# POOL splits one table part behind its first four lookups, and the indices of the lookups move to ACT's queue

## The reference

```python
e = jnp.stack([tbl_0[ids[:, 0]], ..., tbl_39[ids[:, 39]]], axis=1)      # (512, 40, 32)
iidx, jidx = jnp.triu_indices(40, k=1)                                  # 780 pairs
z = jnp.einsum('bpd,pde,bpe->bp', e[:, iidx, :], bilinear_matrices, e[:, jidx, :])
h = jnp.concatenate([z, dense_ctx], axis=1)                             # (512, 796)
h = jnp.maximum(h @ W_top1 + b_top1, 0.0)                               # 512
h = jnp.maximum(h @ W_top2 + b_top2, 0.0)                               # 256
y = h @ W_top3                                                          # (512, 1)
```

## Time and profile before

| | |
|---|---|
| Median of 3 runs | 193.12 us (193.04 to 193.39) |
| The profiled execution's own time | 193.5 us |
| Its span in the trace | 191.7 us |
| Granted TensorE clock in the span | 1.0 of full speed |
| Busy: PE | 179.4 us (94%) |
| Busy: DVE | 147.5 us (77%) |
| Busy: POOL | 107.0 us (56%) |
| Busy: ACT | 52.9 us (28%) |

### The profile page before, as it was taken

How to read it: one execution, slowest core, us unless ns; L and a number is a source line. 1 busy time by engine, 2 the same in 40 slices (tenths; PEclk the granted TensorE clock), 3 DMA queues, 4 the chain that set the end, 5 groups by cost and what they waited for, 6 DMA issues and landing times.

```text
span 191.7 us, 3810 instructions
## 1 busy us (share of the span) xinstructions
PE 179.4 (94%) x1630; PEld 57.9 (30%) x1630; DVE 147.5 (77%) x147; ACT 52.9 (28%) x52; POOL 107.0 (56%) x114
## 2 busy tenths in 40 slices
PE   6688598899999999999999999999999999998992
PEld 6433232233313222222232223222222323222340
DVE  1899989997689979668699969686969987663502
ACT  3879496894100210211110111102011011112501
POOL 2678777878777777777777777779020002222000
PEclk9999999999999999999999999999999999999999
DMA  5995212340397410140000000000000000000000
GB/s 142 390 392 222 67 43 33 94 120 12 84 319 261 148 20 14 26 153 13 14 14 17 14 12 15 14 14 10 2 0 3 0 0 0 3 0 2 3 0 0
DMA packets 7609, 12.89 MB, mean 67 GB/s; under 512 B 2068, under 2 KB 4504, under 8 KB 7592
## 3 DMA queue, kind: packets, MB, share of 16 engines
q1 hardware_dynamic: 4520, 11.07, 16.9%
q0 software_dynamic: 3072, 1.58, 4.6%
HBM read 12.64 MB, written 0.00 MB: 66 GB/s over the span
## 4 chain that ended last, share of the span: by engine, by line
PE 86%; DVE 7%; DMA 2%; issue 2%; ACT 1%; DVEq 0%
PE ps_t L637 29%; PE ps_z L651 26%; PE ps_x L675 11%; PE ps_t L631 5%; PE ps_t L686 4%; DVE hot_dve L516 4%; PE ps_x L601 4%; PE ps_t L601 3%; DMA ids<-ids_oh 2%; PE ps_t L660 2%; DVE late_w L523 2%; PE ps_x L613 2%; PE ps_z L601 1%; DVE tbl_last L526 1%; DVE prod L556 1%
## 5 line engine op out<-in xcount | busy, mean ns | idle before, releaser
L556 DVE TENSOR_TENSOR prod<-ps_t,xt 128x1024 f32<-128x1024 f32 x100 | 115.7, 1217 | 25.5 <-PE ps_t L637 22.1
L446 POOL DMA_INDIRECT emb<-tbl,idx x96 | 95.8, 998 | 32.8 <-issue 29.0
L637 PE MATMUL ps_t<-xt,w_sb 32*128 32x512 f32 x360 | 58.6, 640 | 0.0
L651 PE MATMUL ps_z<-prod,ones 128*32 128x512 f32 x400 | 53.0, 604 | 0.0
L454 POOL TENSOR_TENSOR late_z<-late_z,tbl_oh 128x512 f32<-128x512 f32 x8 | 10.1, 1279 | 36.2 <-ACT tbl_oh L497 36.2
L637 PEld LDWEIGHTS ps_t<-xt,w_sb 32*128 32x128 f32 x360 | 19.8, 183 | 34.2 <-issue 21.0
L675 PE MATMUL ps_x<-late_z,late_w 128*32 128x512 f32 x192 | 22.8, 592 | 0.0
L516 DVE TENSOR_SCALAR hot_dve<-ids,ramp 128x2048 bf16<-128x2048 int16 x26 | 18.1, 745 | 3.7 <-DMA ids<-ids_oh 3.7
L651 PEld LDWEIGHTS ps_z<-prod,ones 128*32 128x32 f32 x400 | 8.1, 108 | 37.9 <-issue 31.0
L469 ACT ACTIVATE hot_act<-ids,neg_ramp 128x2048 bf16<-128x2048 int16 x8 | 15.9, 1992 | 3.0 <-DMA ids<-ids_oh 3.0
L497 ACT ACTIVATE tbl_oh<-ps_x 128x512 f32<-128x512 f32 x8 | 4.8, 597 | 40.7 <-PE ps_x L675 40.7
(11 more groups left out here) (62 smaller groups left out, 86.8 us busy)
## 6 DMA issues: line engine op xcount, KB each, us to landing
ids<-ids_oh SPq DMA_DIRECT2D x4, 512.0 KB, 7.0
emb<-tbl,idx POOLq DMA_INDIRECT x96, 2.4
late_w<-w SPq DMA_DIRECT2D x1, 1280.0 KB, 10.3
tbl_oh<-small_tables SPq DMA_DIRECT2D x2, 512.0 KB, 8.7
late_w<-w SPq DMA_DIRECT2D x2, 512.0 KB, 4.9
w_sb<-w_pairs SPq DMA_DIRECT2D x1, 704.0 KB
tbl_oh<-small_tables SPq DMA_DIRECT2D x1, 640.0 KB
w_sb<-w_pairs SPq DMA_DIRECT2D x1, 640.0 KB
```

The costliest lines, as they stand in the source:

```text
L446: nc.gpsimd.indirect_dma_start(emb[:, n % E_RING, t, u * D:(u + 1) * D], None, tables[field], bass.IndirectOffsetOnAxis(ap=idx[:, at:at + ...
L556: nc.vector.tensor_tensor(prod[:, g % PROD_RING, :].rearrange("p (i b) -> p i b", i=2), ps_t[PAIR[g]][:, :].rearrange("p (i b) -> p i b", ...
L637: last = nc.tensor.matmul(o, w_sb[s * D:(s + 1) * D, at:at + P], xt[s * D:(s + 1) * D, kk, :], start=True, stop=True)
L651: last = nc.tensor.matmul(ps_z[q * D:(q + 1) * D, :], ones[:, v * D:(v + 1) * D], prod[:, t // 2 % PROD_RING, t % 2 * B:(t % 2 + 1) * B], ...
```

## The change

Four things change.

- The two subtractions of table part 3 move from DVE to POOL, which does them behind its fourth lookup, when the part has landed. They have semaphores of their own, `tbl_rest_pool` and `tbl_last_pool`, and PE waits for the latter ahead of hot (2, 0).
- DVE splits part 4 behind the step hot (2, 3), and no longer behind hot (2, 7).
- The load of `idx` is issued by ACT, as its first instruction, and no longer by SP.
- The counts of the waits are renumbered, since DVE makes four parts.

```diff
+POOL_PART, POOL_LOOKUPS = 3, 4
+DVE_PARTS = [n for n in range(len(TBL_PARTS)) if n != POOL_PART]
...
-SPLIT_AT = {(0, 3): 1, (1, 3): 2, (2, 7): 3}
+SPLIT_AT = {(0, 3): 1, (2, 3): 3}
...
             load_small_ids(0)
-            sp.dma_start(idx[:, :], ids).then_inc(ids_in, 16)
             load_small_tables(0)
...
+            def split_part():
+
+                cols = part_cols(POOL_PART)
+                pool.wait_ge(tbl_in[POOL_PART], 16)
+                nc.gpsimd.tensor_tensor(tbl_rest[:, cols], tbl_oh[:, cols], upper_halves(tbl_oh[:, cols]),
+                                        ALU.subtract).then_inc(tbl_rest_pool, 1)
+                pool.wait_ge(tbl_rest_pool, 1)
+                nc.gpsimd.tensor_tensor(tbl_last[:, cols], tbl_rest[:, cols], upper_halves(tbl_rest[:, cols]),
+                                        ALU.subtract).then_inc(tbl_last_pool, 1)
+
             pool.wait_ge(ids_in, 16)
+            lookups = 0
             for n, k in enumerate(looked_up):
...
                             bass.IndirectOffsetOnAxis(ap=idx[:, at:at + 1], axis=0)).then_inc(gathered[k], 16)
+                        lookups += 1
+                        if lookups == POOL_LOOKUPS:
+                            split_part()
...
+            act.dma_start(idx[:, :], ids).then_inc(ids_in, 16)
             act.wait_ge(ramp_made, len(OH_BLOCKS))
...
-                dve.wait_ge(tbl_rest_made, n + 1)
+                dve.wait_ge(tbl_rest_made, DVE_PARTS.index(n) + 1)
...
-                        pe.wait_ge(tbl_last_made, PART_OF_BLOCK[j] + 1 if j else 1)
+                        if PART_OF_BLOCK[j] == POOL_PART:
+                            pe.wait_ge(tbl_last_pool, 1)
+                        else:
+                            pe.wait_ge(tbl_last_made, DVE_PARTS.index(PART_OF_BLOCK[j]) + 1 if j else 1)
```

More of the change, by code:

```diff
@@ L346, in dlrm_tower @@
         tbl_rest_made, tbl_last_made = sem("tbl_rest_made"), sem("tbl_last_made")
+        tbl_rest_pool, tbl_last_pool = sem("tbl_rest_pool"), sem("tbl_last_pool")
         hot_made_dve, hot_made_act = sem("hot_made_dve"), sem("hot_made_act")
```

## The result

The changed kernel takes 198.68 us (median of 4 runs, 197.25 to 199.39), the kernel before 193.19 us beside it; ratio 1.027 (95% interval 1.024 to 1.031), 5.2 us slower by the ratio. The forecast was 198.0 us. The profiled execution of after is the shortest of the four: 197.25 us, span 195.4 us, 3.7 us more than before. The other three lie at 198.57 to 199.39 us, at a mean granted clock of 0.981 to 0.983. None of these three left a trace; the experiments come back to this gap.

The account below looks back on a forecast made before the run. PE sets the pace from 31.7 us; before that a chain through DVE binds. DVE held 2 x 2.4 us plus 0.1 us gives 193.5 + 4.9 = 198.4 us, less 0.4 us for the median: 198.0 us, range 193.3 to 199.0 us.

Parts of the forecast that it names:

- What bounds, and what is late next: Block 2: PE's 1.93 us wait for DVE is no prize, since ACT's one-hot pair ends at 30.15 us, PE's meeting 30.20.
- The exclusion: Block 1's start: DVE stands for the whole of both POOL subtractions, 4.8 us, read from POOL's lookups standing behind DVE.
- Rivals 1 and 2: 1: POOL does not hold DVE up, 192.8 to 194.3 us, chance 0.25; 2: DVE goes first, 196.1 to 198.6 us, 0.08.
- rival 3: Partial: only one subtraction excludes, or accesses are dealt out in turn; +1 to +3.5 us, 194.1 to 196.6 us, chance 0.09.
- the fourth: Table lands so late that POOL works behind block 1's one-hots, around 20 us; +2 to +5 us, no chance of its own.
- the sum: Block 1: two DVE one-hots held 2.4 us each plus 0.1 us handing over, 4.9 us late, carried to the end.
- POOL's duration: POOL's two 128x1024 subtractions: 2.4 us each, 4.8 us together, from a range of 2.25 to 2.56 us.
- the sign that the prediction named: Profile after: POOL's two 128x1024 instructions of 2.3 to 2.6 us begin at the end of a DVE instruction.
- The indices: Load on ACT's queue: earlier indices gain 0, sharing engines with the first ids costs at most 0.4 us; taken as 0.
- The argument of equal bytes: Indices and first ids at the head are the same bytes together, so moving the load's issue was taken as 0.
- The band of 197.3 to 198.8 us: Forecast case for the whole kernel, said to follow from POOL's 2.25 to 2.56 us; chance 0.58.
- What moves along: Part 4's early split has 0.5 to 1 us of cover, block 3's lookups 2 us; PE's wait on POOL's part 0.

Follow-up runs that it names:

- the half-size run: Against the kernel with only the split on POOL: POOL's two subtractions made on 128x512, PE reading the first half's for the second half; 195.09 us, ratio 1.009.
- the later place: Against the kernel with only the split on POOL: POOL's split put behind its tenth lookup in place of its fourth; 196.78 us, ratio 1.018.
- the spare matmuls: Kernel with only the split on POOL, plus 10 and 4 identity matmuls on PE ahead of one-hot matmuls (1, 0) and (1, 1); 197.15 us, ratio 1.022.
- the kernel with ACT relieved: Kernel in which nobody splits part 3, with DVE making one-hot (2, 3) in place of ACT; 191.78 us, then 190.82 us with part 4's split put back late.
- both split: Kernel before, DVE making every split, with POOL repeating the two subtractions into tiles nobody reads; 198.43 us, ratio 1.025.

## Why the prediction was right

**What bounds, and what is late next.** Right, and shown in both directions: no split of part 3 at all gives 0.9996, with PE standing for ACT's pair; with ACT's one-hot and part 4's split moved as well it gives 0.988.

**The exclusion.** Right in kind. The step that the prediction took from one direction of the rows holds: DVE stands for both POOL instructions, for nearly the whole of each (1.6 of 1.9 us), in proportion to their size, and with nobody waiting for their result. The Trainium skill's rule ("SBUF — State Buffer", Who interferes with whom), that the second of the two is blocked and not merely slowed, is borne out for DVE behind POOL as well: 2.38 us for a one-hot that takes 0.75 us. Rivals 1 and 2 fall by the same rows, since DVE did not keep its times and POOL was done at 18.30 us; rival 3, too, since both instructions excluded DVE; and the fourth, since the table had landed by 13.06 us. That is 0.2 us ahead of the 13.3 us that the prediction allowed at the earliest, while DVE's two subtractions came 0.5 us late. So POOL got in between the two and not behind both: what it held up was the second subtraction and one one-hot, where the sum had two one-hots. DVE has no slack in either, so the place cost nothing more.

**POOL's duration.** Mis-sized. I scaled from 128x512 in float32 and took 2.4 us; one such subtraction takes 1.89 us alone and holds DVE for 1.6 us. With that the term is 3.2 us in place of 4.9 us. The 2.41 and 2.75 us in after's profile look like the sign that the prediction named (2.3 to 2.6 us), but by luck: some 0.5 and 0.9 us of them are POOL's own waiting for DVE. The estimate of 2.3 us from the Trainium skill's "GPSIMD Engine Reference" (Elementwise) is for float32 throughout, and is above what this half-bf16 subtraction takes as well; in the half-size run the first subtraction on 128x512 took 1.04 us, where the float32 addition of the earlier trace rows takes 1.28 us.

**The indices.** "I take 0" was the wrong end: the bound of 0.4 us for the shared DMA engines was the right order but too low, and the run with this half alone gives +0.7 us (0.4 to 0.9 us). On top of the split it shows less: 5.2 us with both, 5.0 us with the split alone. The argument of equal bytes failed, and not because the indices went ahead of the ids: they landed later too, 5.1 us after an issue that came 0.4 us earlier, in place of 4.2 us. Why both loads came later is open. In the Trainium skill, "DMA: Bandwidth & Descriptors" (Issuing engines are not separate DMA queues) has it that DMAs from all engines interleave on the same 16 DMA engines; the trace agrees, with 198 packets of SP's queue and 134 of ACT's in the first 5 us, and the first ids landed 0.5 us later.

**What was missing.** The price of a PE that stands. Behind the new wait its granted clock falls to 0.50 to 0.55 in four experiments, and DVE's first product then waits 1.6 to 1.8 us for it in place of 0.17 us in three of them (at the fourth, the later place, the second product waits 2.54 us); the spread of after's runs (197.25 us at clock 1.0, 198.57 to 199.39 us at 0.981 to 0.983) agrees with it, though the latter left no trace. So 198.0 us came close by luck, with errors of opposite sign: 1.7 us too much for POOL, and some 2 us left out. Terms as the runs size them give 3.2 + 0.5 + 1.5 = 5.2 us, but this sum was made afterwards: its 1.5 us is the delay of the first product without the spare matmuls (22.14 less 20.64 us), and after's profiled execution shows none of it, and a loss of 3.7 us. The band of 197.3 to 198.8 us was luck too: with POOL's 2.25 to 2.56 us, from which it is said to come, the sum gives 197.7 to 198.3 us, and the measured 198.68 us lies above that.

**What moves along.** The lookups were covered (the transposition moved with all else, with no wait of its own). The early split of part 4 cost nothing in after, as predicted, since group 4 waited for ACT's copy; in the kernel with ACT relieved it cost about 1 us (191.78 to 190.82 us), so its cover was thin, as the prediction said with its 0.5 to 1 us.

## What to carry to other kernels

Before work goes from DVE to POOL to relieve DVE, look at what DVE runs beside it: here each POOL instruction of 1.9 us took 1.6 us out of DVE, to spare it one of 1.2 us, and only DVE's products from PSUM ran beside POOL untouched. Before anything is taken off an engine, follow its consumer to the next wait; a meeting of two engines within 0.05 us, as PE's with ACT, means that to relieve one of them alone can be worth nothing, as it was here for DVE. And a new wait of some 2 us on PE can cost more than itself, since PE may come back at half its rate.

## What the runs showed of the hardware, unexpected

- In after's profile PE's matmuls in block 0 run at half their rate, four every 0.43 us from 8.59 to 14.1 us in place of every 0.215 us, while the column of the granted clock has 1.00 for these stretches; PE had stood 2.01 us. In the run with the indices alone on ACT's queue the same stretch is recorded with 0.50 (8 to 10 us). So matmul spacing is the surer sign, and a mean clock near 1.0 doesn't prove that PE ran at its full rate throughout.
- The clock did not fall at every such wait: after's profiled execution has PE standing 2.15 us ahead of block 1 (19.00 us) and full rate behind it; with 2.33 us (split only) it fell, with 2.22 us (half the size) and 3.35 us (both split) too, and at the later place behind stands of only 1.26 and 1.47 us. So the length of the last stand alone doesn't decide it; what does, nothing here settles.

```profile
8.59 0.62 PE L622 MATMUL ps_x<-hot_dve,tbl_oh 125*32 125x512 bf16 x4 [2.01 <-DVE tbl_last L544]
8.99 0.65 PE L622 MATMUL ps_x<-hot_dve,late_w 125*32 125x512 bf16 x4
...
14.52 0.39 PE L622 MATMUL ps_x<-hot_dve,tbl_last 125*32 125x512 bf16 x4
14.74 0.39 PE L622 MATMUL ps_x<-hot_dve,tbl_oh 125*32 125x512 bf16 x4
```
